# Gathering every second expert tile as quarter rows and turning it on VectorE in 32x32 blocks, in an attention and mixture-of-experts layer on one core

## Chip, core and metric

The kernel runs on one core of a Trainium2 chip. The metric is device time in microseconds (us) for one execution. The engines are TensorE (PE for its matmuls, PEld for its weight loads), VectorE (DVE), ScalarE (ACT), GpSimd (POOL) and the queue of SyncE (SP), which issues the plain DMAs. GpSimd issues the indirect DMAs, which gather rows by a list of row numbers.

## What is computed

One layer over 8 sequences of 512 tokens with 512 features: a layer norm, then the input plus causal attention with 16 heads plus a mixture of experts in which every token goes to 2 of 8 experts.

```python
x = L0_attn_x                                  # (8, 512, 512) float32
xn = _layernorm(x, axis=-1)
x = x + attn(xn, Wq, Wk, Wv, Wo) + ffn(xn, gate_w, expert_w, expert_b)

# ffn
xf = x.reshape(B * S, D)                       # 4096 tokens
gate_logits = xf @ gate_w.T                    # 8 experts
top_vals, top_idx = jax.lax.top_k(gate_logits, 2)
w = jax.nn.softmax(top_vals, axis=-1)
y_all = jnp.einsum('td,eod->teo', xf, expert_w) + expert_b[None, :, :]
y_sel = jnp.take_along_axis(y_all, top_idx[:, :, None], axis=1)
out = jnp.sum(y_sel * w[:, :, None], axis=1)
```

## The kernel before

The attention is done in 32 steps (a batch and four heads each). Between step 15 and step 16 stands the expert stage, which the change is about. By then VectorE has sorted the tokens: each of the 8192 choices of a token has a slot, the slots of an expert fill whole tiles of 128, and there are `NTILE` = 71 tiles. `tok_of` holds the token in every slot, `exp_of` the expert of every tile. The normalised input lies in memory as `xn_rows`, one row of 512 float32 (2 KB) for each token.

The loop over tiles `s` = 0 to 70 is a pipeline over five engines with four buffers of everything. Nothing in it is scheduled by a planner: each engine has its own program, written in a fixed order, and waits on semaphores.

- POOL, `gather_x(s)` (L603 to L611): one indirect DMA fetches the 128 rows of tile s into `x_g[s % 4]`. It waits until tile s-4 has been read from that buffer (`xg_turned`).
- PE, `turn_xg(s)` (L930 to L939, the transposes are at L926): four 128x128 float32 transposes of `x_g` into a PSUM bank.
- ACT, `high_xg(s)` (L786), reads that bank and writes the high float16 half of `x_gT`. DVE, `low_xg(s)` (L1439), subtracts and writes the low half.
- PE, `expert(s)` (L949): 12 matmuls of 128x512 float16 (four chunks of features, three products of halves) with the expert's weights `w_exp`, which lie on the chip for all 8 experts.
- DVE, `scale_y(s)` (L1453): scale and bias from the PSUM bank into `y_sb`. SP, `store_y(s)` (L526): the tile goes to `y_rows`.

TensorE's program in this stage is the transposes of tile s+1 and then the matmuls of tile s, and so on:

```python
for s in range(NTILE):
    if 0 < s < NTILE - 1:
        turn_xg(s + 1)
    expert(s)
```

VectorE's program is `low_xg(s + 3)` and then `scale_y(s)`, for each s. Because `low_xg(s + 3)` needs the transposes that TensorE makes just ahead of `expert(s + 2)`, VectorE runs about two tiles behind TensorE's matmuls with its `scale_y`. After the stage, POOL gathers the results of the experts back by token (`gather_y`, L620, two indirect DMAs of 128 rows of 2 KB for a tile of tokens), and steps 16 to 31 add them up.

Attention has a block transpose on VectorE already: `turn_blk` (L1429) turns 32x32 blocks of `x_blk` in place, and `normalise_o` has two more (L1499, L1501).

## Time and profile before

| | |
|---|---|
| time before, median of 3 runs | 984.97 us (984.73 to 988.17) |
| the profiled execution: its own time | 987.53 us |
| the profiled execution: its span, first to last instruction | 985.8 us |
| PE busy | 917.9 us, 93% |
| DVE busy | 744.3 us, 76% |
| POOL busy | 561.3 us, 57% |
| ACT busy | 436.6 us, 44% |
| granted clock of TensorE, mean | 0.987 |

The span is the time from the first to the last instruction of the profiled execution. Busy times are sums over the whole span, and they are averages over stages with different limits: the expert stage has to be read by itself, by the instructions of one tile in order of time.

### The profile page before, as it was taken

To read this page: it belongs to the slowest core of one execution; us is meant where nothing else is said; L and a number is where in the kernel's file an instruction comes from. 1 tells how busy PE (TensorE), PEld (TensorE's weight loads), DVE (VectorE), ACT (ScalarE), POOL (GpSimd) and SP (SyncE) were. 2 spreads that over 40 slices of the span, in tenths; PEclk is the share of its full clock that TensorE was granted. 3 is DMA by queue.
4 is the path that set the end of the run, shared out by engine and by line. 5 is a ranking of instruction groups with operands and counts; after the bars stand their busy time and mean duration, and the time that the engine had idled before them with its cause. 6 is when DMAs were issued, how large, how long until landed. Compare 5 with 4: busy or idle time off the path is not lost.

```text
span 985.8 us, 18723 instructions
## 1 busy us (share of the span) xinstructions
PE 917.9 (93%) x6557; PEld 452.1 (46%) x6589; DVE 744.3 (76%) x1327; ACT 436.6 (44%) x711; POOL 561.3 (57%) x553
## 2 busy tenths in 40 slices
PE   2898898999999989989999999989999999999887
PEld 1344344444444544545555555544444444444333
DVE  7988988898789899944444444487788888888865
ACT  5367867766765433431122111124334444344432
POOL 1545676674776446763333333157878888778731
PEclk9999999999999999999999999999999999999999
DMA  6365589688786353485655555464655554565531
GB/s 243 109 223 198 179 269 320 199 306 293 211 275 260 119 204 97 187 291 192 198 176 178 172 171 174 148 214 141 193 177 188 172 194 141 163 189 159 173 103 55
DMA packets 107963, 188.63 MB, mean 191 GB/s; under 512 B 11872, under 2 KB 65248, under 8 KB 102624
## 3 DMA queue, kind: packets, MB, share of 16 engines
q1 hardware_dynamic: 97072, 152.03, 44.4%
q0 software_dynamic: 10800, 35.40, 12.5%
q8 instruction: 56, 0.92, 0.4%
q14 instruction: 35, 0.29, 0.1%
HBM read 117.13 MB, written 70.25 MB: 190 GB/s over the span
## 4 chain that ended last, share of the span: by engine, by line
PE 66%; DVE 14%; DMA 6%; ACT 5%; POOL 4%; issue 3%; SPq 1%; another core or an unknown queue 0%; DVEq 0%; ACTq 0%; POOLq 0%
PE psum L949 19%; PE psum L1034 10%; PE psum L1058 7%; PE psum L997 5%; PE psum L984 5%; PE psum L966 5%; PE psum L1000 5%; PE psum L1043 4%; PE psum L926 4%; DVE top L1483 3%; ACT pT L762 2%; DMA sum_sb<-x 2%; POOL k_hl L590 1%; PE psum L968 1%; DMA w_rows<-w_hl 1%
## 5 line engine op out<-in xcount | busy, mean ns | idle before, releaser
L762 ACT ACTIVATE pT<-psum,factors 128x512 f32<-128x512 f32 (+1 forms) x352 | 218.2, 642 | 244.0 <-PE psum L984 226.8
L1483 DVE TENSOR_REDUCE top<-psum 128x1 f32<-128x384 f32 (+3 forms) x352 | 210.4, 634 | 22.0 <-PE psum L968 16.6
L1034 PE MATMUL psum<-xT,w_att 128*128 128x512 f16 x768 | 195.7, 380 | 6.7 <-DVE xT L1434 4.7
L949 PE MATMUL psum<-w_exp,x_gT 128*128 x852 | 195.3, 379 | 0.6 <-DVE x_gT L1439 0.6
L610 POOL DMA_INDIRECT x_g<-xn_rows,tok_of x71 | 67.5, 951 | 131.5 <-PE psum L926 129.6
L966 PE MATMUL psum<-k_stack,q_stack 96*128 96x384 f16 (+3 forms) x512 | 127.8, 303 | 15.6 <-DVE top L1483 13.0
L984 PE MATMUL psum<-q_stack,k_stack 98*128 98x256 f16 (+3 forms) x512 | 129.5, 306 | 11.0 <-ACT pT L762 8.9
L1439 DVE TENSOR_TENSOR x_gT<-psum,x_gT 128x512 f16<-128x512 f32 x71 | 49.0, 692 | 104.1 <-ACT x_gT L786 90.7
L949 PEld LDWEIGHTS psum<-w_exp,x_gT 128*128 128x128 f16 x852 | 83.4, 98 | 85.5 <-issue 0.9
L786 ACT ACTIVATE x_gT<-psum 128x512 f16<-128x512 f32 x71 | 42.3, 597 | 170.0 <-PE psum L926 170.0
L600 POOL TENSOR_TENSOR o_hl<-o_sb,o_hl 128x512 f16<-128x512 f32 x31 | 36.5, 1178 | 127.9 <-ACT o_hl L776 123.2
L1034 PEld LDWEIGHTS psum<-xT,w_att 128*128 128x128 f16 x768 | 70.0, 97 | 73.6 <-DVE xT L1434 5.1
L594 POOL TENSOR_SCALAR_AFFINE_SELECT pT<-pT 128x512 f32<-128x512 f32 x128 | 95.1, 753 | 11.7 <-ACT pT L762 11.6
L1058 PE MATMUL psum<-w_att,o_hl 128*128 128x512 f16 x384 | 100.2, 386 | 1.3 <-DVE o_hl L1520 1.3
L1043 PE MATMUL psum<-w_att,xT 128*128 128x512 f16 x384 | 98.1, 380 | 0.0
L997 PE MATMUL psum<-pT,v_sb 128*32 128x512 f32 (+1 forms) x992 | 92.7, 446 | 0.0
L1000 PE MATMUL psum<-pT,ones 128*32 128x512 f32 (+1 forms) x992 | 91.5, 441 | 0.0
L966 PEld LDWEIGHTS psum<-k_stack,q_stack 96*128 96x128 f16 x512 | 46.5, 98 | 69.1 <-DVE top L1483 32.0
L620 POOL DMA_INDIRECT y_in<-y_rows,idx_y x64 | 66.8, 1043 | 19.7 <-issue 11.6
L968 PE MATMUL psum<-causal,ident 128*128 128x128 bf16 (+1 forms) x320 | 74.2, 232 | 0.0
L984 PEld LDWEIGHTS psum<-q_stack,k_stack 98*128 98x128 f16 x512 | 44.3, 98 | 64.1 <-ACT pT L762 18.1
L585 POOL TENSOR_TENSOR turned_q<-turned_q,trig_sb 128x512 f32<-128x512 f32 x32 | 40.6, 1270 | 42.7 <-DVE plain_q L1468 42.7
(175 smaller groups left out, 1301.9 us busy)
## 6 DMA issues: line engine op xcount, KB each, us to landing
y_rows<-y_sb SPq DMA_DIRECT2D x71, 256.0 KB
w_in<-w_all SPq DMA_DIRECT2D x12, 1024.0 KB, 12.1
q_stack<-qk_rows SPq DMA_DIRECT2D x96, 128.0 KB
k_stack<-qk_rows SPq DMA_DIRECT2D x96, 128.0 KB
x_in<-x SPq DMA_DIRECT2D x8, 1024.0 KB, 10.2
qk_rows<-q_hl SPq DMA_DIRECT2D x32, 256.0 KB
qk_rows<-k_hl SPq DMA_DIRECT2D x32, 256.0 KB
xn_rows<-x_in SPq DMA_DIRECT2D x8, 1024.0 KB, 5.0
```

The source lines that it names most:

```text
L594: pool.affine_select(out=p_diagonal(j), in_=p_diagonal(j), compare_op=ALU.is_ge, fill=0.0, base=0, pattern=[[0, HG], [1, P]], channel_mult ...
L762: act.activation(p_of(j, h, heads), banks[BANK_T + (NT_ * n + k) % 2][:, 0:W], ACT.Exp, scale=factors[:, 0:1]).then_inc(exp_done, 1)
L949: now = pe.matmul(banks[s % 4], x_gT[s % 4][:, xp * C + c, :], w_exp[:, bass.ds(e, 1), wp, c, :].rearrange("p e d -> p (e d)"), start=n == ...
L966: pe.matmul(bank[:, h * W:(h + 1) * W], q_stack[u][0:ROW_C, h0 + h, i * P:(i + 1) * P], k_stack[u][0:ROW_C, h0 + h, 0:W], start=h == 0, st ...
L968: pe.matmul(bank[:, 0:heads * W].rearrange("p (h t) -> p h t", h=heads)[:, :, W - P:W], ident16[:], causal[:, 0:heads, :], start=False, st ...
L984: now = pe.matmul(bank[:, h * W:(h + 1) * W], k_stack[u][0:ROW_C + 2, h0 + h, j * P:(j + 1) * P], q_stack[u][0:ROW_C + 2, h0 + h, j * P:S] ...
L997: pe.matmul(banks[BANK_O][h * HD:(h + 1) * HD, j * P:S], v_sb[b % 2][:, j, g * P + h * HD:g * P + (h + 1) * HD], p_of(j, h, 1), start=j == ...
L1000: now = pe.matmul(banks[BANK_DEN][h * HD:(h + 1) * HD, j * P:S], ones32[:], p_of(j, h, 1), start=j == 0, stop=j == J - 1)
L1034: now = pe.matmul(bank, w_att[:, what, wp, c, g * P:(g + 1) * P], xT[b % 2][:, xp * C + c, :], start=at_pass == 0, stop=at_pass == 3 * C - 1)
L1043: now = pe.matmul(banks[bank], xT[b % 2][:, xp * C + c, j * P:(j + 1) * P], w_att[:, 2, wp, c, :], start=at_pass == 0, stop=at_pass == 3 * ...
L1058: now = pe.matmul(banks[bank], o_hl[b % 2][:, c, xp, j * P:(j + 1) * P], w_att[:, 3, wp, c, :], start=at_pass == 0, stop=at_pass == 3 * C - 1)
L1483: return dve.tensor_reduce(out=top[:, h:h + heads, i], in_=banks[BANK_S + k % 2][:, 0:heads * W].rearrange("p (h t) -> p h t", h=heads), a ...
```

## The change

Tiles 5, 7, 9, ... 69 (33 tiles, `BLK`) no longer go through TensorE's transposes. `xn_rows` is seen as quarter rows of 128 float32 (`xn_quarters`). For such a tile POOL issues four indirect DMAs instead of one. Each fetches 128 quarter rows of 512 bytes, so that partition q*32+r holds quarter q of 32 tokens. One `dve.transpose` in 32x32 blocks then turns the tile in place. ACT and DVE take the high and low halves from `x_g` itself, in SBUF, with a stride of four elements. The weights of the experts are laid out by the host so that the features match, and the transposes of the other tiles read with the same stride. The buffer `x_g` of such a tile comes free with `low_xg` and not with the transposes of TensorE.

The list of quarter rows (`tok_blk`) is made once: POOL builds a spreading matrix `four16` in step 13, TensorE spreads the tokens with four small matmuls ahead of tile 0 (`spread_tokens`), and VectorE writes the list (`block_tokens`).

```diff
+    FIRST_BLK = 5
+    BLK = list(range(FIRST_BLK, NTILE, 2))
...
+    xn_quarters = xn_rows.rearrange("t (a f) -> (t a) f", f=P)
...
             def gather_x(s):
                 u = s % 4
-                if s >= 4:
-                    pool.wait_ge(xg_turned, s - 3)
+                if s - 4 in BLK:
+                    pool.wait_ge(xg_lo, s - 3)
+                elif s >= 4:
+                    pool.wait_ge(xg_turned, rows_till(s - 4))
...
-                pool.indirect_dma_start(x_g[u][:], None, xn_rows, bass.IndirectOffsetOnAxis(ap=tok_of[:, s:s + 1], axis=0))\
-                    .then_inc(gathered[u], 16)
+                if s in BLK:
+                    if s == FIRST_BLK:
+                        pool.wait_ge(blk_done, 1)
+                    i = BLK.index(s)
+                    for t in range(P // HD):
+                        pool.indirect_dma_start(x_g[u][:, t * P:(t + 1) * P], None, xn_quarters,
+                                                bass.IndirectOffsetOnAxis(ap=tok_blk[:, t, i:i + 1], axis=0)).then_inc(gathered[u], 16)
+                else:
+                    pool.indirect_dma_start(x_g[u][:], None, xn_rows, bass.IndirectOffsetOnAxis(ap=tok_of[:, s:s + 1], axis=0))\
+                        .then_inc(gathered[u], 16)
...
+                if n == CHOOSE + 2:
+                    pool.wait_ge(chosen_done, 1)
+                    pool.tensor_copy(four16[:], ident16[:].rearrange("p (t r) -> p t r", r=HD).unsqueeze(2).broadcast_to([P, P // HD, C, HD]))\
+                        .then_inc(four_made, 1)
...
             def high_xg(s):
-                act.wait_ge(xg_turned, s + 1)
+                if s in BLK:
+                    act.wait_ge(xg_blocked, blks_till(s))
+                else:
+                    act.wait_ge(xg_turned, rows_till(s))
...
+                if s in BLK:
+                    act.activation(by_chunks(x_gT[s % 4][:, 0:C, :]), of_blocks(x_g[s % 4][:]), ACT.Copy).then_inc(xg_hi, 1)
...
+            def spread_tokens():
+                pe.wait_ge(four_made, 1)
+                pe.wait_ge(tok16_done, 1)
+                for t in range(P // HD):
+                    now = pe.matmul(banks[BANK_T + 1][:, t * len(BLK):(t + 1) * len(BLK)],
+                                    four16[:, t, :, :].rearrange("p a r -> p (a r)"),
+                                    tok16[:, FIRST_BLK:NTILE:2], start=True, stop=True)
+                now.then_inc(blk_spread, 1)
...
+            spread_tokens()
             for s in range(NTILE):
-                if 0 < s < NTILE - 1:
+                if 0 < s < NTILE - 1 and s + 1 not in BLK:
                     turn_xg(s + 1)
                 expert(s)
...
+                if s in BLK:
+                    hi, lo = (by_chunks(x_gT[s % 4][:, h * C:(h + 1) * C, :]) for h in range(2))
+                    dve.tensor_tensor(lo, of_blocks(x_g[s % 4][:]), hi, ALU.subtract).then_inc(xg_lo, 1)
...
+            def turn_xg_blocks(s):
+                dve.wait_ge(gathered[s % 4], got(s))
+                here = x_g[s % 4][:].rearrange("p (t r c) -> p t c r", c=C, r=HD)
+                dve.transpose(here, here).then_inc(xg_blocked, 1)
...
             def read_tokens():
                 dve.wait_ge(tok_summed, 1)
+                dve.tensor_copy(tok16[:], banks[BANK_QV][:, 0:NTILE]).then_inc(tok16_done, 1)
...
             for s in range(NTILE):
+                if s + 4 in BLK:
+                    turn_xg_blocks(s + 4)
                 if s + 3 < NTILE:
                     low_xg(s + 3)
```

On POOL, the place is the start of the expert stage. Before, the rows after `o_hl` are the gathers of tiles 4, 5, 6, 7 and 8, one DMA each:

```order
L600 TENSOR_TENSOR o_hl_105<-o_sb,o_hl_105 128x512 [waits o_hi]
L610 DMA x_g_120<-xn_rows,tok_of 128x512 [waits xg_turned]
L610 DMA x_g_121<-xn_rows,tok_of 128x512 [waits xg_turned]
L610 DMA x_g_122<-xn_rows,tok_of 128x512 [waits xg_turned]
L610 DMA x_g_123<-xn_rows,tok_of 128x512 [waits xg_turned]
L610 DMA x_g_120<-xn_rows,tok_of 128x512 [waits xg_turned]
```

With the change the same place reads as follows. The rows are those of tiles 4 to 7 (L649 is the line of a whole-row gather now, L646 that of the quarter rows, and `small_sb` holds the list `tok_blk`):

```order
L629 TENSOR_TENSOR o_hl_107<-o_sb,o_hl_107 128x512 [waits o_hi]
L649 DMA x_g_122<-xn_rows,tok_of 128x512 [waits xg_turned]
L646 DMA x_g_123<-xn_rows,small_sb 128x128 [waits blk_done,xg_turned]
L646 DMA x_g_123<-xn_rows,small_sb 128x128 x3
L649 DMA x_g_124<-xn_rows,tok_of 128x512 [waits xg_turned]
L646 DMA x_g_125<-xn_rows,small_sb 128x128 [waits xg_turned]
L646 DMA x_g_125<-xn_rows,small_sb 128x128 x3
```

Two tiles are five DMAs on POOL's queue where they were two. The gathers keep their order, and each whole-row gather stands behind the four of the tile ahead of it.

On DVE, the place is the first two turns of the loop. Before, after the last `normalise_o`, `low_xg(2)`, `low_xg(3)` and the scale of tile 0:

```order
L1504 TENSOR_TENSOR o_sb<-psum,rden 128x512 [waits o_lo,dve_own]
L1439 TENSOR_TENSOR x_gT_130<-psum,x_gT_130 128x512 [waits xg_hi]
L1439 TENSOR_TENSOR x_gT_131<-psum,x_gT_131 128x512 [waits xg_hi]
L1447 TENSOR_LOAD exp_of [waits bias_loaded]
L1447 ISA x2
L1453 ISA [waits q_stored,y_done]
L1453 SCALAR_TENSOR_TENSOR y_sb_124<-psum,down,bias_all 128x512
```

With the change there is the list of quarter rows (L1516) ahead of tile 2, and the block transpose of tile 5 (L1512) ahead of the low half of tile 4:

```order
L1583 TENSOR_TENSOR o_sb<-psum,rden 128x512 [waits o_lo,dve_own]
L1516 TENSOR_SCALAR small_sb<-psum,small_sb 128x132 [waits blk_spread]
L1507 TENSOR_TENSOR x_gT_132<-psum,x_gT_132 128x512 [waits xg_hi]
L1507 TENSOR_TENSOR x_gT_133<-psum,x_gT_133 128x512 [waits xg_hi]
L1526 TENSOR_LOAD exp_of [waits bias_loaded]
L1526 ISA x2
L1532 ISA [waits q_stored,y_done]
L1532 SCALAR_TENSOR_TENSOR y_sb_126<-psum,down,bias_all 128x512
L1512 STREAM_TRANSPOSE x_g_123<-x_g_123 128x4x4x32 [waits gathered1]
L1507 TENSOR_TENSOR x_gT_130<-psum,x_gT_130 128x512 [waits xg_hi]
```

So VectorE now waits for a gather itself, and while it waits for tile s+4, the low half of tile s+3 and the scale of tile s stand behind it.

## Rows read from the trace of the kernel before

**Rows 1.** The page, busy time of each engine over the span.

```profile
PE 917.9 (93%) x6557; PEld 452.1 (46%) x6589; DVE 744.3 (76%) x1327; ACT 436.6 (44%) x711; POOL 561.3 (57%) x553
```

**Rows 2.** Stretches of the expert stage: PE, PEld, DVE, ACT, POOL busy, PEclk, DMA, GB/s.

```profile
500.00:550.00 50.00, 50.00 (x266) 27.08 (x264) 24.18 (x34) 9.55 (x16) 15.35 (x17) 1.00 0.53 172
```

**Rows 3.** Timeline, about one tile in the steady state: start, us, instruction, idle before.

```profile
504.43 0.60 PE L926 MATMUL psum<-ident,x_g 128*128 128x128 f32 x4
...
504.87 2.75 PE L949 MATMUL psum<-w_exp,x_gT 128*128 x12
505.07 0.60 ACT L786 ACTIVATE x_gT<-psum 128x512 f16<-128x512 f32 x1 [2.43 <-PE psum L926]
505.30 0.95 POOL L610 DMA_INDIRECT x_g<-xn_rows,tok_of  x1 [2.08 <-PE psum L926]
505.70 0.69 DVE L1439 TENSOR_TENSOR x_gT<-psum,x_gT 128x512 f16<-128x512 f32 x1 [1.43 <-ACT x_gT L786]
506.54 0.75 DVE L1453 SCALAR_TENSOR_TENSOR y_sb<-psum,down,bias_all 128x512 f32<-128x512 f32 x1 [0.15 <-issue]
...
507.46 0.60 PE L926 MATMUL psum<-ident,x_g 128*128 128x128 f32 x4
...
507.89 2.75 PE L949 MATMUL psum<-w_exp,x_gT 128*128 x12
```

**Rows 4.** The chain that ended last, end of the stage: start, us, what.

```profile
641.23 5.19 PE psum L949 x24
```

**Rows 5.** Timeline of POOL at the start of the stage.

```profile
436.33 0.96 POOL L610 DMA_INDIRECT x_g<-xn_rows,tok_of  x1
437.60 0.95 POOL L610 DMA_INDIRECT x_g<-xn_rows,tok_of  x1 [0.30 <-issue]
438.85 0.95 POOL L610 DMA_INDIRECT x_g<-xn_rows,tok_of  x1 [0.30 <-issue]
```

**Rows 6.** Line L620, the gathers of y: duration in ns, then the time to landing.

```profile
L620 POOL DMA_INDIRECT y_in<-y_rows,idx_y x64: 945/978/1363, 650.3 to 953.8; - x64
...
DMA to landing us min/median/max: 3.3/3.6/4.2
```

**Rows 7.** The queues between 430 and 647 us: packets, MB, share of 16 engines.

```profile
q0 software_dynamic: 5446, 17.84, 28.4%
```

**Rows 8.** Tile x_blk: SP loads in 512-byte pieces, VectorE's block transpose, ScalarE's reading.

```profile
L1429 DVE STREAM_TRANSPOSE x_blk<-x_blk x24: 662/694/711, 115.7 to 282.0; 128x512 f32<-128x512 f32 x24
L718 ACT ACTIVATE gT<-x_blk x24: 612/612/631, 121.0 to 285.2; 128x512 f16<-128x512 f32 x24
...
DMA to landing us min/median/max: 3.7/4.7/6.9
```

**Rows 9.** Timeline of POOL: gathers beside VectorE's instructions of rows 10.

```profile
676.80 0.99 POOL L620 DMA_INDIRECT y_in<-y_rows,idx_y  x1 [0.27 <-POOL idx_y L618]
...
690.52 1.36 POOL L620 DMA_INDIRECT y_in<-y_rows,idx_y  x1 [0.27 <-POOL idx_y L618]
...
935.38 1.10 POOL L620 DMA_INDIRECT y_in<-y_rows,idx_y  x1 [0.31 <-issue]
```

**Rows 10.** Timeline of DVE at the same times.

```profile
677.35 0.71 DVE L1501 STREAM_TRANSPOSE rden<-rden_few 128x512 f32<-128x512 f32 x1
...
690.24 0.75 DVE L1528 SCALAR_TENSOR_TENSOR late_sb<-y_in,w,late_sb 128x512 f32<-128x512 f32 x1
...
934.92 0.75 DVE L1527 SCALAR_TENSOR_TENSOR late_sb<-y_in,w,late_sb 128x512 f32<-128x512 f32 x1
```

**Rows 11.** Timeline around the small additions: step 13, the token list, tile 0.

```profile
365.72 1.16 POOL L600 TENSOR_TENSOR o_hl<-o_sb,o_hl 128x512 f16<-128x512 f32 x1 [12.08 <-ACT o_hl L776]
...
406.55 0.23 DVE L1443 TENSOR_SCALAR tok_of<-psum 128x71 int32<-128x71 f32 x1 [0.77 <-PE psum L919]
...
432.22 2.76 PE L949 MATMUL psum<-w_exp,x_gT 128*128 x12 [0.61 <-DVE x_gT L1439]
...
444.33 2.75 PE L949 MATMUL psum<-w_exp,x_gT 128*128 x12
```

More of the change, by code:

```diff
@@ L89, in moe_attention_layer @@
     tile_no = small_sb[:, NT * E:NT * E + NTILE]
+    quarter = small_sb[:, NT * E + P:NT * E + P + 1]
     count16 = at("count16", [P, P], F16)
@@ L97, in moe_attention_layer @@
     tok_of = at("tok_of", [P, NTILE], I32)
+    tok16 = at("tok16", [P, NTILE], F16)
     exp_of = at("exp_of", [P, NTILE], I32)
@@ L114, in moe_attention_layer @@
     shift = at("shift", [P, 2, J], F32)
+    logit_at = place[0]
     logit = at("logit", [P, NT, E], F32)
+    four16 = at("four16", [P, P // HD, C, HD], F16, logit_at)
+    tok_blk = small_sb[:, 0:P // HD * len(BLK)].bitcast(I32).rearrange("p (t s) -> p t s", t=P // HD)
+    assert P // HD * len(BLK) <= NT * E and 2 * C * P <= 4 * NT * E
     best = at("best", [P, 2, NT], F32)
@@ L226, in moe_attention_layer @@
     tok_summed, tok_done, bias_loaded = sem("tok_summed"), sem("tok_done"), sem("bias_loaded")
+    four_made, tok16_done, blk_spread, blk_done, xg_blocked = (sem(n) for n in ("four_made", "tok16_done", "blk_spread", "blk_done", "xg_blocked"))
     gathered = [sem(f"gathered{u}") for u in range(4)]
@@ L288, in moe_attention_layer, with rows_till, blks_till, got @@
     HALF_LAST = [(BANK_O, BANK_DEN), (BANK_T, BANK_T + 1)]
+    def rows_till(s):
+        return s + 1 - blks_till(s)
+    def blks_till(s):
+        return len([i for i in BLK if i <= s])
+    def got(s):
+        return sum(64 if i in BLK else 16 for i in range(s % 4, s + 1, 4))
     def outs_till(n):
@@ L328, in by_blocks, with by_chunks, of_blocks @@
         return row.rearrange("p (t r) -> p t r", r=HD)
+    def by_chunks(part):
+        return part.rearrange("p c (t r) -> p c t r", r=HD)
+    def of_blocks(rows):
+        return rows.rearrange("p (t r c) -> p c t r", c=C, r=HD)
     def spread_at(i):
@@ L785, in high_xg @@
                     act.wait_ge(pv_done, J * N1)
-                act.activation(x_gT[s % 4][:, 0:C, :].rearrange("p c t -> p (c t)"), banks[BANK_QV + s % 4], ACT.Copy).then_inc(xg_hi, 1)
+                if s in BLK:
+                    act.activation(by_chunks(x_gT[s % 4][:, 0:C, :]), of_blocks(x_g[s % 4][:]), ACT.Copy).then_inc(xg_hi, 1)
+                else:
+                    act.activation(x_gT[s % 4][:, 0:C, :].rearrange("p c t -> p (c t)"), banks[BANK_QV + s % 4], ACT.Copy).then_inc(xg_hi, 1)
             def step(n):
@@ L938, in turn_xg @@
                     pe.wait_ge(o_read, N1)
-                turn_tile(x_g[s % 4][:], BANK_QV + s % 4).then_inc(xg_turned, 1)
+                rows = x_g[s % 4][:].rearrange("p (f c) -> p c f", c=C)
+                for k in range(C):
+                    now = pe.transpose(banks[BANK_QV + s % 4][:, k * P:(k + 1) * P], rows[:, k], ident32[:])
+                now.then_inc(xg_turned, 1)
             def expert(s):
@@ L945, in expert @@
                     pe.wait_ge(y_scaled, s - 3)
+                elif s == BANK_T + 1:
+                    pe.wait_ge(blk_done, 1)
                 n = 0
@@ L1714, in by_turned_features, with by_strided_features @@
         return w.T.reshape(C, C, P // C, w.shape[0]).transpose(0, 2, 1, 3).reshape(P, C, w.shape[0])
-    mats = [chunks(a["L0_ffn_expert_w"][e]) for e in range(E)]
+    def by_strided_features(w):
+        return w.T.reshape(P, C, w.shape[0])
+    mats = [by_strided_features(a["L0_ffn_expert_w"][e]) for e in range(E)]
     mats += [by_turned_features(a["L0_attn_" + n]) for n in ("Wq", "Wk", "Wv")] + [chunks(a["L0_attn_Wo"])]
@@ L1725 @@
     small = np.concatenate([np.tile(E - np.arange(E), T // P), np.arange(P)]).astype(np.float32)
+    small = np.tile(small, (P, 1))
+    quarter = (D // P * (T // 2) + np.arange(P)[:, None] // (P // C)).astype(np.float32)
     arrays = {
@@ L1731 @@
         "trig": trig,
-        "small": np.tile(small, (P, 1)),
+        "small": np.concatenate([small, quarter], axis=1),
     }
```

10 lines of the change are left out of this document (8 added, 2 removed).

## Prediction, made before the change was run

> **What bounds the kernel now.** I read the busy shares first, then the expert stage by itself. TensorE is busy for 93% of the span and VectorE for 76% [rows 1]. Those are averages over stages. In the middle of the expert stage PE is busy for 50.00 of 50 us at the full granted clock, VectorE for 24.18, ScalarE for 9.55 and POOL for 15.35, and the DMA engines for 0.53 [rows 2]. The timeline says what PE does. The matmuls of one tile begin at 504.87 and those of the next at 507.89, 3.02 us later. Four transposes begin at 504.43, 0.44 us before the matmuls, and at 507.46, 0.43 before [rows 3]. So a tile costs PE about 2.59 us of matmuls and 0.44 of transposes, and nobody keeps it waiting: POOL idles 2.08 us ahead of each gather, ScalarE 2.43. The stage runs from 432.22, where tile 0 begins [rows 11], to 641.23 + 5.19 = 646.42 [rows 4].
>
> **What goes from the path.** 33 tiles lose their transposes: 33 x 0.44 = 14.5 us. That is the ceiling of the gain. Two tiles would take 2 x 3.02 - 0.44 = 5.6 us of PE in place of 6.04. Everything else has to fit into 5.6 us for two tiles.
>
> **What is added on POOL.** Two tiles are five indirect DMAs where they were two. At the start of the stage three gathers go out with nothing to wait for. They begin at 436.33, 437.60 and 438.85, and each runs 0.95 us with 0.30 us of issue between them [rows 5]. A gather thus takes POOL 1.25 us. The gathers of y are of the same kind, 128 rows of 2 KB, with a median of 0.978 us [rows 6]. Five of them are 6.25 us for two tiles. This is more than the 5.6 of PE with the change, and more than the 6.04 of today. POOL's average of 57% hides it, since it waits for most of each tile now.
>
> The open price is that of a quarter-row gather. No row shows one of 512-byte rows. From above I take 1.25 us, because the number of rows (128) and of indices is the same and the work of making the descriptors goes by these. Of a lower price I can only say that 0.30 us of issue stays. If the busy part went by bytes it would be 0.95 / 4 = 0.24, so that the lower end is 0.54 us. I take 1.25. The Trainium skill (DMA: Bandwidth & Descriptors, "Anatomy of one DMA — SWDGE (gpsimd) path") calls descriptor generation "small, variable" and says that many descriptors can be emitted before it shows, with some 2.0 us fixed for a DMA. By the page alone POOL would not be the limit and the sum would be the gain of the second case below; the 0.95 us of the row is what this kernel pays, so I go by the row.
>
> **The sum.** POOL begins tile 4 at 436.33 as before. Until the last quarter of tile 69 it starts 1 gather for tile 4, 33 x 4 = 132 quarters and 32 whole ones for tiles 6 to 68. The last of these 165 starts 164 x 1.25 = 205.0 us later, at 641.33. It lands 3.6 us after its issue [rows 6], at 644.9. VectorE then turns the tile in 0.69 [rows 8] and makes the low half of tile 68, which stands behind that transpose on its queue, in 0.69 [rows 3]. With about 0.06 for each semaphore tile 68 can begin at 646.5. Three tiles of matmuls and one set of transposes follow, 3 x 2.59 + 0.44 = 8.2, so the stage ends at 654.7, against 646.42: **+8.3 us**. It begins at once: the last quarter of tile 5 starts at 441.3 and lands at 444.9, and the low half of tile 4 follows at 446.4, where PE wanted it at 444.33 [rows 11].
>
> **VectorE beside POOL.** Half of the low-half subtractions now read two tensors in SBUF (x_g and the high half). A gather beside such an instruction is longer. One took 1.36 us (0.95 otherwise) where L1528 had begun 0.28 us before it and ran 0.47 us into it; one took 1.10 where L1527 ran 0.29 us into it [rows 9, 10]. The block transpose from SBUF to SBUF (L1501) does not do this: the gather at 676.80 took 0.99 [rows 9, 10]. There is one such subtraction for two tiles. When it falls between the starts of two gathers it costs nothing, and when it lies over one as in the worst row it costs 0.41. I take 0.15, near the row in which a third of a microsecond overlaps: 33 x 0.15 = **+5.0 us**, between 0 and 13.5. The Trainium skill (SBUF — State Buffer, "SBUF: two separate sides") gives a rule for it: the one of VectorE and GpSimd that comes second is blocked until the other's instruction ends. The trace agrees roughly. By the rule at its worst it would be the whole 0.69 us each time, 22.8 us in all, which no row here shows.
>
> **What is hidden.** The block transpose (0.69) makes VectorE's work for two tiles 24.18 / 50 x 6.04 + 0.69 = 3.6 us [rows 2], well under 6.25, and ScalarE's reading from SBUF takes 0.61 [rows 8], as from PSUM. If either were twice as long it would still fit. The spreading matrix on POOL in step 13 lies in the 12.08 us that POOL waits there [rows 11]. The four small matmuls ahead of tile 0 fall into the 0.61 us that PE waits for x_gT [rows 11]. The one small copy ahead of `tok_of` is on PE's path: 0.15 to 0.23 us [rows 11], say **+0.15**. The DMA engines: a gather of 256 KB now takes 0.284 x 16 x 217 / 67 = 14.7 engine-us, 0.92 us of all sixteen [rows 7]. In small pieces it may be twice that, 1 us more in 6.25, on a share of 0.53: no bound.
>
> In all 8.3 + 5.0 + 0.15 = +13.4 us. On the profiled execution that is a span of 985.8 + 13.4 = 999.2, with 1.7 us around it. The median lies 2.6 us below that execution's time, so the forecast is 984.97 + 13.4 = **998.4 us**.
>
> **The cases.**
> - *POOL is the bound* (0.67). 993.4 with no collision between VectorE and POOL, 1006.9 with the worst row at each pair. For it speaks the pitch of 1.25 us; against it only that quarter rows were not seen.
> - *Cheap quarter gathers* (0.15), the other sign: POOL keeps up and PE stays the bound. This decides at the price of one gather. The stage is even with today's at 1.25 - 8.3 / 164 = 1.20 us a gather without a collision, and PE is the bound from about 5.6 / 5 = 1.12 us down. At 1.0 us or less the gain is 14.5 less about 2 for the wait for tile 5's quarters at the start: 972.5 us. For it speaks that only a quarter of the bytes is described.
> - *In between* (0.06): a pitch of 1.16 to 1.21 us, 980 to 990.
> - *The ring is too short* (0.12). A quarter tile holds its buffer for three pitches (3.75), the landing, the transpose, the low half of the tile ahead, the scale and its own low half, about 7 us besides the landing. Four buffers give it two pairs, 12.5 us, so up to a landing of 5.5 us it costs nothing. Loads in 512-byte pieces landed in 3.7, 4.7 and 6.9 us at the least, the median and the most [rows 8]. At the median nothing changes but 1 us at the end; at 6.9 a pair would take (7 + 6.9) / 2 = 6.95 us, 0.7 more, and the time would be 1016 to 1022. A sign of this would be gaps on POOL.
>
> **How the numbers follow.** A measurement of this kernel tells about 0.5%, 4.9 us, from no change. Faster than 980 us: the second case and a little of the third, 0.16. Between 980 and 990: the rest of the third and a sliver of the first, 0.06. Slower: the first and the fourth, 0.78. The range goes from 986 to 1015 us: it holds the first case with its bounds of 0 and 13.5 us, half of the third, and the milder half of the fourth, about 0.8 in all, and leaves the second out.
>
> **What would show it.** In the stage, gathers of quarter rows on POOL at a pitch of 1.25 us with "issue" in front of each and no wait for PE or DVE; POOL near 76% busy there; PE with a wait of about half a microsecond or more ahead of every second tile, released by DVE's low half; two tiles in 6.3 to 6.6 us where it was 6.04; a wait of VectorE for the gathers' landing; PE and the clock elsewhere as before. A wrong first step would be a quarter gather clearly under 0.95 us busy. A wrong second step would be POOL waiting for `xg_lo` or for PE in the middle of the stage. A granted clock of 1.2 GHz in the stage, where it is 2.4 now, would make it worse than all of these.

## The result and the profile after

The change made the kernel slower: 1011.95 us (median of 4 runs, 1007.78 to 1015.55) against 986.57 us (median of 4 runs, 984.73 to 990.37). The ratio is 1.0242, 95% interval 1.0201 to 1.0284, which is about +23.9 us (the two medians lie 25.4 us apart). The forecast was 998.4 us, +13.4. The direction and the range (986 to 1015) held, the size of the change did not. The profiled execution took 1015.55 us, the most of the four, so what is read from its trace below is the costly end of what this kernel does.

The page of the changed kernel, span and busy times:

```profile
span 1013.8 us, 18572 instructions
## 1 busy us (share of the span) xinstructions
PE 915.7 (90%) x6429; PEld 441.1 (44%) x6461; DVE 783.9 (77%) x1362; ACT 454.2 (45%) x711; POOL 671.0 (66%) x653
```

TensorE is busy for 2.2 us less and the span is 28 us longer. POOL went from 57% to 66% [rows 1]. Part 4 of the same page, the chain that ended last by line:

```profile
POOL x_g L646 11%; PE psum L1097 10%; PE psum L1121 6%; PE psum L1060 5%; PE psum L1047 5%; PE psum L1029 5%; PE psum L1063 4%; PE psum L1012 4%; PE psum L1106 4%; DVE top L1562 3%; POOL x_g L649 3%; DMA c_rows<-c_turn 2%; DMA x_blk<-xn_rows 1%; POOL gT L610 1%; PE psum L1031 1%
```

The gathers of quarter rows (L646) head the chain now. In the kernel before, the expert matmuls (L949) stood there with 19%, and no gather of x_g was among the first lines. The matmuls (L1012) have shrunk to 4%.

```profile
PE psum L949 19%; PE psum L1034 10%; PE psum L1058 7%; PE psum L997 5%; PE psum L984 5%; PE psum L966 5%; PE psum L1000 5%; PE psum L1043 4%; PE psum L926 4%; DVE top L1483 3%; ACT pT L762 2%; DMA sum_sb<-x 2%; POOL k_hl L590 1%; PE psum L9
```

The timeline of POOL at the start of the stage, in the changed kernel, answers to [rows 5]:

```profile
444.19 0.97 POOL L649 DMA_INDIRECT x_g<-xn_rows,tok_of  x1
445.46 0.94 POOL L646 DMA_INDIRECT x_g<-xn_rows,small_sb  x1 [0.30 <-issue]
446.71 0.94 POOL L646 DMA_INDIRECT x_g<-xn_rows,small_sb  x1 [0.30 <-issue]
447.96 0.94 POOL L646 DMA_INDIRECT x_g<-xn_rows,small_sb  x1 [0.30 <-issue]
449.20 0.94 POOL L646 DMA_INDIRECT x_g<-xn_rows,small_sb  x1 [0.30 <-issue]
450.45 0.95 POOL L649 DMA_INDIRECT x_g<-xn_rows,tok_of  x1 [0.30 <-issue]
...
460.53 1.75 POOL L646 DMA_INDIRECT x_g<-xn_rows,small_sb  x1 [0.30 <-issue]
```

A gather of 512-byte rows takes 0.94 us, one of 2 KB rows 0.95, and both have 0.30 us of issue in front. POOL's pitch is 1.25 us and it waits for nobody. The last row is one of the gathers that took longer, 1.75 us. In the timeline of VectorE of the changed kernel at that time stands what ran beside it:

```profile
458.10 1.14 DVE L1512 STREAM_TRANSPOSE x_g<-x_g 128x512 f32<-128x512 f32 x1 [1.73 <-DMA x_g<-xn_rows,small_sb]
459.12 0.66 DVE L1507 TENSOR_TENSOR x_gT<-psum,x_gT 128x512 f16<-128x512 f32 x1
459.69 0.75 DVE L1532 SCALAR_TENSOR_TENSOR y_sb<-psum,down,bias_all 128x512 f32<-128x512 f32 x1
460.44 1.08 DVE L1505 TENSOR_TENSOR x_gT<-x_g,x_gT 128x512 f16<-128x512 f32 x1
461.43 0.74 DVE L1532 SCALAR_TENSOR_TENSOR y_sb<-psum,down,bias_all 128x512 f32<-128x512 f32 x1
```

The subtraction with two inputs in SBUF (L1505) began at 460.44, 0.09 us before the gather, and ended at 461.52. The gather ended at 462.28, 0.76 us after it. So the gather had done about 0.2 us of its work beside or before the wait and the rest afterwards: it lost 0.8 us. Where L1505 begins after the start of a gather, the gather takes 0.94. Here is such a pair, POOL and VectorE:

```profile
467.57 0.94 POOL L646 DMA_INDIRECT x_g<-xn_rows,small_sb  x1 [0.30 <-issue]
467.63 1.07 DVE L1505 TENSOR_TENSOR x_gT<-x_g,x_gT 128x512 f16<-128x512 f32 x1
```

This holds through the whole stage. From 450 us on, 25 gathers took longer than 0.98 us. Each had begun inside a subtraction L1505, and each ended 0.76 to 0.78 us after it. Two more began inside one and were not longer, one 0.03 us after the subtraction's start and one near its end. The 13 gathers in which a subtraction began took 0.94 to 0.95. Those subtractions took 1.06 to 1.08 us like all others, with no idle time in front: VectorE was never held up.

These are the groups of the stage, by line and form (engine, operation, count, busy, mean ns, idle before):

```profile
L646 POOL DMA_INDIRECT x_g<-xn_rows,small_sb x132 | 139.4, 1056 | 40.2 <-issue 40.2
L649 POOL DMA_INDIRECT x_g<-xn_rows,tok_of x36 | 34.9, 970 | 10.7 <-issue 9.9 <-PE psum L999 0.6
...
L1512 DVE STREAM_TRANSPOSE x_g<-x_g 128x512 f32<-128x512 f32 x33 | 37.3, 1130 | 83.9 <-DMA x_g<-xn_rows,small_sb 83.9
L1505 DVE TENSOR_TENSOR x_gT<-x_g,x_gT 128x512 f16<-128x512 f32 x33 | 35.4, 1073 | 0.1
```

The quarter gathers have a mean of 1056 ns and a median of 944 (below, with the third experiment). 132 x 0.112 = 14.8 us went into the gathers that were held up, and 36 x 0.024 = 0.9 more into those of whole rows. POOL's idle time here is its own issue, all but 0.6 us behind PE. VectorE's transpose and subtraction take 1.13 and 1.07 us where the forecast had 0.69 for each: both read x_g with a stride of four elements. The granted clock of TensorE was 0.99 in the mean from 440 to 678 us, the level of 2.4 GHz for nearly all of the stage, so a lower clock is not what made it long.

TensorE in the changed kernel, the line of the expert matmuls (first and last start, then what it waited for):

```profile
L1012 PE MATMUL psum<-w_exp,x_gT x852: 378/379/635, 440.4 to 677.6; 128*128 x171
...
  issue: 46.5, 42
  DVE x_gT L1507: 28.3, 20
```

From the first to the last of these matmuls it is 237.2 us. In the kernel before it was 646.0 - 432.2 = 213.8 us (432.22 in [rows 11], and the last matmul starts 0.4 before the end, 646.42, of [rows 4]). That is +23.4 us in the stage. The rest of this text calls this distance "the stage". The stage also begins 8.2 us later than before. From the start of the last matmul to the end of the span it is 3.6 us less than before (336.2 and 339.8). The experiments ask which part of this is the change.

### The profile page after: what moved, and what is told of

The parts are those of the page before. It is cut to its first block, busy times and chain, and to the rows that moved or that the text cites. A ratio compares the mean times of both kernels' runs of the same rounds, so it can differ in the third digit from the quotient of the medians.

```text
span 1013.8 us, 18572 instructions
## 1 busy us (share of the span) xinstructions
PE 915.7 (90%) x6429; PEld 441.1 (44%) x6461; DVE 783.9 (77%) x1362; ACT 454.2 (45%) x711; POOL 671.0 (66%) x653
## 4 chain that ended last, share of the span: by engine, by line
PE 48%; POOL 18%; DVE 15%; issue 7%; DMA 5%; ACT 4%; SPq 1%; another core or an unknown queue 0%; DVEq 0%; ACTq 0%; POOLq 0%
POOL x_g L646 11%; PE psum L1097 10%; PE psum L1121 6%; PE psum L1060 5%; PE psum L1047 5%; PE psum L1029 5%; PE psum L1063 4%; PE psum L1012 4%; PE psum L1106 4%; DVE top L1562 3%; POOL x_g L649 3%; DMA c_rows<-c_turn 2%; DMA x_blk<-xn_rows 1%; POOL gT L610 1%; PE psum L1031 1%
## 5 line engine op out<-in xcount | busy, mean ns | idle before, releaser
L1012 PE MATMUL psum<-w_exp,x_gT 128*128 x852 | 197.7, 384 | 29.1 <-DVE x_gT L1507 28.3
L646 POOL DMA_INDIRECT x_g<-xn_rows,small_sb x132 | 139.4, 1056 | 40.2 <-issue 40.2
L1012 PEld LDWEIGHTS psum<-w_exp,x_gT 128*128 128x128 f16 x852 | 84.2, 99 | 128.1 <-issue 45.9
L1047 PE MATMUL psum<-q_stack,k_stack 98*128 98x256 f16 (+3 forms) x512 | 129.2, 304 | 10.5 <-ACT pT L805 8.1
L1512 DVE STREAM_TRANSPOSE x_g<-x_g 128x512 f32<-128x512 f32 x33 | 37.3, 1130 | 83.9 <-DMA x_g<-xn_rows,small_sb 83.9
L835 ACT ACTIVATE x_gT<-psum 128x512 f16<-128x512 f32 x38 | 22.6, 597 | 110.2 <-PE psum L999 110.2
## 6 DMA issues: line engine op xcount, KB each, us to landing
x_in<-x SPq DMA_DIRECT2D x8, 1024.0 KB, 10.5
```

The costliest lines, as they stand in the source:

```text
L646: pool.indirect_dma_start(x_g[u][:, t * P:(t + 1) * P], None, xn_quarters, bass.IndirectOffsetOnAxis(ap=tok_blk[:, t, i:i + 1], axis=0)).t ...
L1012: now = pe.matmul(banks[s % 4], x_gT[s % 4][:, xp * C + c, :], w_exp[:, bass.ds(e, 1), wp, c, :].rearrange("p e d -> p (e d)"), start=n == ...
L1047: now = pe.matmul(bank[:, h * W:(h + 1) * W], k_stack[u][0:ROW_C + 2, h0 + h, j * P:(j + 1) * P], q_stack[u][0:ROW_C + 2, h0 + h, j * P:S] ...
```

## Experiments

Each kernel below was compared with the kernel before on the same chip. That kernel's median was 987.6 to 988.9 us in these comparisons, so the ratios, not the times, compare one experiment with another.

**e1: the kernel before, again.** No edit.

> The kernel before, run again with a profile of its own. In the two profiles so far tile 0 of the expert stage begins at 432.22 us before and at 440.39 us with the change, 8.2 us of the lost time ahead of the stage. If that is chance of an execution (landing times of DMAs in steps 3 to 10), this profile may show tile 0 anywhere from 432 to 440 us; if the change causes it, tile 0 is within 1 us of 432.2 here and near 440 in every kernel with the changed memory layout. The ratio is 1.000 within 0.4%.

Ratio 1.0029 (1.0003 to 1.0056), tile 0 at 435.26 us. Two things follow. The start of the stage moves by 3 us (432.2 and 435.3) between executions of one and the same kernel. And an identical kernel can come out 0.3% off, so a single difference of 0.3% shows nothing here.

**e2: quarter gathers replaced by whole ones.** It leaves out the right place of the rows, so the values of the 33 tiles are other than the reference's.

```diff
-                    i = BLK.index(s)
-                    for t in range(P // HD):
-                        pool.indirect_dma_start(x_g[u][:, t * P:(t + 1) * P], None, xn_quarters,
-                                                bass.IndirectOffsetOnAxis(ap=tok_blk[:, t, i:i + 1], axis=0)).then_inc(gathered[u], 16)
+                    pool.indirect_dma_start(x_g[u][:], None, xn_rows, bass.IndirectOffsetOnAxis(ap=tok_of[:, s:s + 1], axis=0))\
+                        .then_inc(gathered[u], 16)
```

> The changed kernel, but each tile of BLK is fetched by one indirect DMA of whole rows and not by four of quarter rows; the VectorE transpose, the list of quarter rows and everything else stay. The rows then stand in the wrong partitions for the transpose, so the values of these tiles are not the reference's. Theory POOL (the gathers' pitch of 1.25 us, with the stretched ones, is what ends last): POOL needs 2.5 us for two tiles, PE is the bound again with 5.65 us for two tiles, the stage takes 200 to 203 us where it takes 237.6, and the time is 970 to 976 us. Rival VectorE (its transposes of 1.13 us, the strided subtraction of 1.08 us and ScalarE's strided 1.13 us make the lateness): these stay, PE still waits ahead of every second tile, and the time stays above 995 us.

980.57 us, ratio 0.9932 (0.9902 to 0.9962). The line of the matmuls in this kernel, and that of the gathers of the 33 tiles:

```profile
L1010 PE MATMUL psum<-w_exp,x_gT x852: 379/379/387, 440.0 to 640.6; 128*128 x171
...
  issue: 1.2, 2
```

```profile
L644 POOL DMA_INDIRECT x_g<-xn_rows,tok_of x33 | 31.1, 941 | 72.6 <-DVE x_gT L1503 72.0 <-issue 0.6
```

The stage is 200.6 us, 13.2 less than before, and PE waits 1.2 us in all of it. VectorE's long transposes (median 1135 ns) and subtractions (1067 ns) are all still there, and POOL is the one that waits now, for VectorE. So the five gathers for two tiles make the loss in the stage, and the transposes on VectorE are covered. How much of it is their number and how much the held-up ones, e2 does not say, since both went. The theory of VectorE falls. The time of 980.6 was above the 970 to 976 expected, though, and the excess lies ahead of the stage, which begins at 440.0.

**e3: the block transpose writes to PSUM.** Every second tile as in the change, with four gathers.

```diff
             def turn_xg_blocks(s):
...
-                dve.transpose(here, here).then_inc(xg_blocked, 1)
+                there = banks[BANK_QV + s % 4].rearrange("p (c t r) -> p t c r", c=C, r=HD)
+                dve.transpose(there, here).then_inc(xg_blocked, 1)
```

`high_xg` and `low_xg` read the bank for these tiles too, and `gather_x` waits for `xg_blocked` where it waited for `xg_lo`.

> The changed kernel, but VectorE's block transpose writes into the PSUM bank that TensorE's transposes would have written. ScalarE and VectorE then read contiguous PSUM as for the other tiles, and VectorE has no instruction with two inputs in SBUF in this stage. The gathers stay as they are. Theory collision: the gathers of 1.5 to 1.8 us go, all of them take 0.94 to 0.95, two tiles take 6.25 us, the stage 222 to 224 us (14 to 16 less than with the change), and the time is 993 to 999 us. Rival ring (the landing and the waits on VectorE set the pace, the long gathers only fill a wait): the long gathers go, POOL shows waits in their place, and the time falls by less than 5 us.

998.01 us, ratio 1.0117 (1.0075 to 1.0159). The line of the gathers, in the changed kernel and in this one (duration min/median/max):

```profile
L646 POOL DMA_INDIRECT x_g<-xn_rows,small_sb x132: 940/944/1798, 445.5 to 664.7; - x132
```

```profile
L646 POOL DMA_INDIRECT x_g<-xn_rows,small_sb x132: 940/944/954, 439.5 to 643.1; - x132
...
L1009 PE MATMUL psum<-w_exp,x_gT x852: 379/379/388, 434.3 to 656.6; 128*128 x171
```

The longest gather fell from 1798 to 954 ns, and the stage from 237.2 to 222.3 us. That is 14.9 us, nearly the 15.7 us of surplus in the gathers. What is left, 222.3 - 213.8 = 8.5 us, is the forecast's first term (8.3). The theory of the ring falls: POOL kept its pace, and the waits for landing did not take the place of the long gathers. This version also gives the buffer back sooner. That is not the gain, since POOL hardly waited for a buffer in the changed kernel either (0.6 us).

**e4: only every third tile, transposed to PSUM.**

```diff
-    BLK = list(range(FIRST_BLK, NTILE, 2))
+    BLK = list(range(FIRST_BLK, NTILE, 3))
```

> As the transpose into PSUM, but only every third tile (5, 8, ... 68, 22 tiles) is gathered as quarter rows. Three tiles cost POOL 6 x 1.25 = 7.5 us and PE 3 x 3.03 - 0.44 = 8.65 us. Theory POOL: PE is the bound, the stage takes 214 - 22 x 0.44 = 204.5 us and up to 2 more at its start, and the time is 975 to 979 us, faster than before. Rival: the gathers' landing or VectorE keeps PE waiting ahead of every third tile all the same, and the time is 984 us or more.

987.19 us, ratio 0.9986 (0.9965 to 1.0007), where 975 to 979 us was expected. The stage is 643.8 - 435.9 = 207.9 us where 204.5 to 206.5 was expected. POOL waits for PE here, and PE hardly waits. The timeline of PE at the start of this kernel's stage shows where the rest went:

```profile
442.00 2.75 PE L1009 MATMUL psum<-w_exp,x_gT 128*128 x12
444.59 0.63 PE L996 MATMUL psum<-ident,x_g 128*128 128x128 f32 x4
445.06 2.75 PE L1009 MATMUL psum<-w_exp,x_gT 128*128 x12
449.79 2.76 PE L1009 MATMUL psum<-w_exp,x_gT 128*128 x12 [1.98 <-DVE x_gT L1500]
```

A tile with transposes takes 445.06 - 442.00 = 3.06 us and not 3.02: the transposes read x_g with the stride and take 0.63 - 0.60 = 0.03 us more, on every tile that keeps them. The wait of 1.98 us is that of tile 4, behind the quarters of tile 5, as forecast. The gain in the stage, 5.9 us, is in the trace, but the time was not below that of before. The profiled execution (983.06 us, the fastest of ten) had tile 0 at 435.9. That the others lost the gain ahead of the stage was a guess at this point, and the next experiments test it.

**e5: the additions alone.**

```diff
-    BLK = list(range(FIRST_BLK, NTILE, 2))
+    COLS = list(range(FIRST_BLK, NTILE, 2))
+    BLK = []
```

with `len(COLS)` in the making of the list.

> All that the change adds around the tiles, but no tile goes the new way: the spreading matrix in step 13, the float16 copy of the tokens, the four small matmuls, the list of quarter rows, the expert weights in their new order and TensorE's transposes with the stride of four elements; every tile is gathered whole and transposed by TensorE. The strided transposes cost 3.06 us a tile in place of 3.03 (read from the starts of the tiles with the change), 71 x 0.03 = 2.2 us. Theory chance: the later start of the expert stage (440.4 and 440.0 us in two of four changed kernels, 432.2 and 435.3 in the two profiles of before) is chance of an execution, and the time is 2 to 3 us above before. Rival systematic: something in these additions makes steps 3 to 10 slower, the stage begins at 436 to 440 us, and the time is 5 to 9 us above before.

996.92 us, ratio 1.0081 (1.0062 to 1.0101), +8.0 us, with tile 0 at 438.2 us and a stage of 654.3 - 438.2 = 216.1 us. The stage holds 2.3 us of it, the stride in TensorE's transposes. This is the rival's number. The rest, over 5 us, is not chance.

**e6: the memory layout alone.** No instruction is added.

```diff
+    tok16 = at("tok16", [P, NTILE], F16)
...
-        "small": np.tile(small, (P, 1)),
+        "small": np.concatenate([np.tile(small, (P, 1)), np.zeros((P, 1), np.float32)], axis=1),
```

> The kernel before, with only the memory layout of the change: the unused 160 bytes for the float16 tokens in each partition, which move every later tile in SBUF, and one more column in the array of small constants, which moves what lies behind it in memory. No instruction is added. Theory chance: no difference, 0.997 to 1.003. Rival systematic by layout: the stage begins near 438 us and the time is 3 us or more above before.

993.29 us, ratio 1.0051 (1.0033 to 1.0069), tile 0 at 437.98. The rival held. The two lines move every later tile of SBUF by 192 bytes in each partition, 160 for `tok16` and 32 for the longer `small_sb`.

**e7: two tiles of five, to PSUM, from tile 8 on.** With the list of tiles made of two lists with a step of 5.

```diff
-    FIRST_BLK = 5
-    BLK = list(range(FIRST_BLK, NTILE, 2))
+    FIRST_BLK = 8
+    PARTS = [list(range(FIRST_BLK + k, NTILE, 5)) for k in (0, 2)]
+    BLK = PARTS[0] + PARTS[1]
```

> Two tiles of five (8, 10, 13, 15, ... 70, 26 tiles) as quarter rows, turned into PSUM, from tile 8 on in place of tile 5. Five tiles cost POOL 11 x 1.25 = 13.75 us and PE 5 x 3.06 - 2 x 0.47 = 14.36 us. Theory POOL: PE is the bound, the stage has no stall near tile 4, and takes 71 x 3.06 - 26 x 0.47 = 205 us, 9 less than before; the time is 976 to 984 us by what the steps ahead of the stage do. Rival ring: the share of POOL (96%) leaves no room for landing and queue, PE waits ahead of many tiles, and the stage takes 212 us or more.

983.48 us, ratio 0.9945 (0.9924 to 0.9966). The stage is 646.3 - 441.6 = 204.7 us, as expected, 9.1 less than before, with the shifted layout still in it.

**e8: no stride.** The three instructions read x_g in order, so the features of these tiles are in the wrong order and the values are other than the reference's.

```diff
-        return rows.rearrange("p (t r c) -> p c t r", c=C, r=HD)
+        return rows.rearrange("p (c t r) -> p c t r", c=C, r=HD)
...
-                here = x_g[s % 4][:].rearrange("p (t r c) -> p t c r", c=C, r=HD)
+                here = x_g[s % 4][:]
```

> The changed kernel with every second tile, turned in place in SBUF, but VectorE's transpose, ScalarE's copy and VectorE's subtraction read x_g without the stride of four elements, so the features of these tiles are in another order than the weights want and the values are not the reference's. Theory collision by length: the three instructions fall from 1.13, 1.13 and 1.08 us to about 0.69, 0.61 and 0.69; the subtraction with two inputs in SBUF still holds up a gather, but by at most 0.45 us instead of 0.85, and the stage is 229 to 233 us where it was 237.6 (and 222 with the transpose into PSUM). Rival: the stride costs in itself, as lateness on VectorE, and not by the gathers; then the stage falls to 224 us or less.

1005.81 us, ratio 1.0165 (1.0137 to 1.0192). Groups of this kernel in the stage:

```profile
L646 POOL DMA_INDIRECT x_g<-xn_rows,small_sb x132 | 129.7, 983 | 40.2 <-issue 40.2
...
L1512 DVE STREAM_TRANSPOSE x_g<-x_g 128x512 f32<-128x512 f32 x33 | 23.5, 711 | 104.7 <-DMA x_g<-xn_rows,small_sb 104.7
L1505 DVE TENSOR_TENSOR x_gT<-x_g,x_gT 128x512 f16<-128x512 f32 x33 | 22.3, 677 | 0.0
```

Without the stride the subtraction takes 0.68 us, and the surplus in the quarter gathers is 132 x 0.039 = 5.1 us in place of 14.8. This is near the forecast's 5.0 us. The stage is 668.9 - 442.9 = 226.0 us, less than the 229 to 233 expected and more than the rival's 224. Against the change the stage lost 11.2 us and the gathers' surplus 10.5, so the held-up gathers explain nearly all of it, and I had set them too high here.

**e9 and e10: the two halves of the layout.** The pad of 160 bytes alone, and the column in memory alone (not loaded).

```diff
+    tok16 = at("tok16", [P, NTILE], F16)
```

```diff
-            sp.dma_start(small_sb[:], small).then_inc(const_in, 16)
+            sp.dma_start(small_sb[:], small[:, 0:small.shape[1] - 1]).then_inc(const_in, 16)
```

> The kernel before with only the unused 160 bytes in each partition of SBUF, half of the layout shift that cost 0.51%. If the place of the tiles in SBUF is the cause: 1.003 to 1.007 and the stage begins near 438 us. If the array of constants is: 0.998 to 1.002.

> The kernel before with only the one more column in the array of small constants in memory, which is not loaded; SBUF is as before. If the place of the arrays in memory is the cause of the 0.51%: 1.003 to 1.007. If it is the place of the tiles in SBUF: 0.998 to 1.002.

The pad: 1.0037 (1.0015 to 1.0058), tile 0 at 438.90. The column: 1.0006 (0.9988 to 1.0023), tile 0 at 432.90. This speaks for the place in SBUF, but by the ratio alone the pad is hardly more than what e1 gave for no edit, and the start of tile 0 is a weak witness. Over all profiles it lies between 434.3 (e3) and 442.9 (e8) with the shifted tiles, and between 432.0 (e14) and 436.0 (e11) with the tiles in place or shifted by 256 bytes. The landings are a better one. Tile x_blk (512-byte pieces loaded by SP), time to landing in the kernel with the pad and in the one with the column:

```profile
DMA to landing us min/median/max: 3.7/5.5/7.7
```

```profile
DMA to landing us min/median/max: 3.4/4.9/7.7
```

**e11: the change with the layout of before.** `tok16` takes the place of `best`, and the number of the quarter is computed on the chip.

```diff
-    tok16 = at("tok16", [P, NTILE], F16)
...
+    tok16 = at("tok16", [P, NTILE], F16, best_at)
...
+            own.link(pool.iota(quarter_i, [[0, 1]], base=D // P * (T // 2) * (P // C), channel_multiplier=1))
...
+            own.link(dve.tensor_scalar(quarter_i, quarter_i, 5, None, ALU.logical_shift_right))
+            own.link(dve.tensor_copy(quarter, quarter_i))
```

> The changed kernel with the memory layout of before: the float16 tokens lie in a tile that is free by then, and the number of the quarter is made on the chip (one iota on POOL, two small VectorE instructions at the start) and not loaded. Theory two causes: the change without the shift of layout loses 4 to 6 us less, 1.017 to 1.021, and the expert stage itself is as long as with the change, 236 to 239 us. Rival: the layout matters only for the kernel before, and the ratio stays at 1.023 or more.

1008.95 us, ratio 1.0192 (1.0157 to 1.0227), within the expectation. The stage was 668.8 - 436.0 = 232.8 us, 4.4 less than with the change, which I had not expected. Its gathers say why:

```profile
L648 POOL DMA_INDIRECT x_g<-xn_rows,small_sb x132 | 134.7, 1021 | 40.2 <-issue 40.2
L651 POOL DMA_INDIRECT x_g<-xn_rows,tok_of x36 | 35.2, 979 | 10.7 <-issue 9.9 <-PE psum L1001 0.6
```

The surplus is 132 x 0.077 + 36 x 0.033 = 11.4 us and not 15.7. In this trace 18 gathers took longer than 0.98 us, in that of the change 25. How many are caught depends on how the two programs meet. With one trace of each kernel it stays open whether that goes with the kernel or with the execution.

**e12: two tiles of five, to PSUM, with the layout of before.** The edits of e7 and e11 together.

> Two tiles of five as quarter rows, turned into PSUM, from tile 8, with the memory layout of before. Theory two causes: the 4 to 6 us of the layout come on top of the gain of 0.55% measured with it, 0.987 to 0.991, 976 to 979 us. Rival: no more gain than with the shifted layout, 0.993 to 0.996.

979.09 us (977.44 to 981.82), ratio 0.9905 (0.9879 to 0.9931), at the upper end of what was expected. This version is faster than both kernels, about 9 us under the one before. Its matmuls and its gathers:

```profile
L1014 PE MATMUL psum<-w_exp,x_gT x852: 378/379/387, 435.0 to 638.8; 128*128 x171
...
  issue: 1.8, 3
```

```profile
L649 POOL DMA_INDIRECT x_g<-xn_rows,small_sb x104 | 98.1, 944 | 40.7 <-issue 27.7 <-PE psum L1001 12.9
```

PE waits 1.8 us in a stage of 203.8 us, and POOL waits for PE now.

**e13 and e14: pads of 128 and 256 bytes.** The kernel before with `place[0] += 128` (256) ahead of `exp_of`.

> The kernel before with 128 unused bytes in each partition. The pads so far were 160 bytes (ratio 1.0037) and, in the full layout shift, 160 + 32 = 192 bytes (1.0051); neither is a multiple of 128, and in both the loads of x_blk landed in 5.5 us where they land in 4.7 to 4.9 with the layout of before. Theory alignment to 128 bytes: 0.998 to 1.002, x_blk in 4.7 to 4.9 us. Rival any shift: 1.003 or more.

> The same with 256 bytes. Theory alignment to 128 bytes: 0.998 to 1.002. If 256 is the step that matters and not 128, this one is at 1.000 and the pad of 128 bytes is not. Rival any shift: both at 1.003 or more.

128 bytes: 1.0029 (1.0008 to 1.0050), x_blk landing in a median of 5.0 us. 256 bytes: 1.0009 (0.9992 to 1.0026), x_blk in 4.8. The pad of 256 bytes shows no loss, so it is not any shift that costs. For 128 bytes the ratio is no larger than that of e1 and tells nothing, but the traces do. These are the plain DMAs' packets, MB and share of the 16 DMA engines between 100 and 300 us: before, with the pads of 128 and 256 bytes, and with that of 160 (e9):

```profile
q1 hardware_dynamic: 34928, 51.51, 77.2%
```

```profile
q1 hardware_dynamic: 35085, 50.63, 79.0%
```

```profile
q1 hardware_dynamic: 35037, 51.78, 77.6%
```

```profile
q1 hardware_dynamic: 34791, 49.30, 79.8%
```

A share of 77.2% of 16 engines for 200 us, divided by 51.51 MB, is 48.0 us of one engine for a MB. It is 49.9 with 128 bytes, 48.0 with 256 and 51.8 with 160. The same rows of all seventeen traces fall into groups that do not touch: 48.0 to 48.4 in the seven kernels with the tiles in place or shifted by 256 bytes, 51.2 to 51.8 in the nine with 160 or 192 bytes, and 128 bytes between them. So with 160 or 192 bytes the DMA engines work about 7% longer for the same bytes, and in this measure 128 bytes costs half as much (one trace). What 128 bytes cost in time stays open.

**e15: every second tile, to PSUM, with the layout of before.** The edits of e3 and e11.

> The change with the transpose into PSUM (no held-up gathers) and with the memory layout of before: what is left is the pitch of the gathers alone. By the forecast's own term for the pitch, +8.3 us, with 0.03 us for each of 38 strided TensorE transposes hidden under POOL: 1.007 to 1.010. If POOL's pitch were not the bound then: 1.003 or less.

995.17 us, ratio 1.0070 (1.0046 to 1.0094). The stage is 654.4 - 432.5 = 221.9 us, +8.1.

## Why the prediction was wrong, step by step

- **The bound and its term: right.** "A gather thus takes POOL 1.25 us" held to the hundredth for quarter rows (0.94 + 0.30). The term was +8.3 us; the two kernels without held-up gathers gave +8.5 (e3) and +8.1 us (e15) in the stage, and e15's time is +0.70% (0.46 to 0.94), 6.9 us. POOL was busy for 38.7 of the 50 us from 480 us, 77% where 76% was named as the sign. PE's waits were fewer and longer than named, 28.3 us at 20 starts and not half a microsecond at every second tile. The wait of tile 4 came as described, and e2 shows that two gathers in place of five turn the loss into a gain. The sentence of the Trainium skill that descriptor generation is small and shows only late (DMA: Bandwidth & Descriptors, "Anatomy of one DMA — SWDGE (gpsimd) path") did not carry here: 0.94 us of POOL for each DMA, with rows of 512 bytes or of 2 KB, is what set the pace.
- **"33 x 0.15 = +5.0 us, between 0 and 13.5": this is the step that failed.** The surplus was 15.7 us in the profiled execution and 11.4 in that of e11. As time it is 1.0192 - 1.0070, 1.2% or 12 us (e11 against e15; with their intervals 8 to 16 us). The mechanism was right and its size was off by more than two times. The bound for one pair, 0.41 us, was too low as well. It came from a gather beside an instruction of 0.75 us that had begun 0.28 us earlier, and here a gather lost up to 0.85 us. The new subtraction takes 1.07 us, since it reads x_g with a stride of four elements, and it often begins just ahead of a gather. So the row of 0.69 us for `low_xg` was the wrong one: it was taken from a contiguous PSUM operand for a strided SBUF operand.
- **How the size could have been worked out.** The forecast took its 0.15 by eye from the overlap. What the traces show is when a held-up gather ends: 0.76 to 0.78 us after the subtraction. The rows of before had this already, with 0.81 and 0.89 us [rows 9, 10]. A gather that begins d us after the subtraction's start then loses 1.07 - d + 0.77 - 0.94 = 0.90 - d. If the subtractions fell anywhere in the pitch of 1.25 us alike, that would be 0.32 us each, 33 x 0.32 = 10.7 us. With 0.68 us and the 0.81 of e8's trace it would be 0.12 each, 4.0 us. These are estimates from the rows named, near the 11.4 of e11 and the 5.1 of e8. So the length of the subtraction explains most of the miss. The 15.7 of the change has bad luck in it: 13 of its 25 long gathers began within 0.1 us of a subtraction's start. That e8 met the forecast's 5.0 is luck in part too, since 0.15 was not worked out from a length.
- **"The block transpose from SBUF to SBUF does not do this": right, but its row did not show it.** The transpose of [rows 10] began 0.55 us after the gather, and a gather that begins first loses nothing in any case. The changed kernel does show it: 17 gathers began inside a transpose L1512 and took 0.94 to 0.95 us.
- **The Trainium skill's rule on the shared ports** (SBUF — State Buffer, "SBUF: two separate sides") gave 22.8 us at its worst with 0.69 us. For a gather that comes second the trace agrees with it more closely than I had allowed: the gather ends 0.76 us after the subtraction, nearly its whole duration. The other half of the rule, as the prediction put it, did not show: a subtraction that began inside a gather took 1.06 to 1.08 us, with no idle time in front.
- **"What is hidden": half right.** The longer transposes and ScalarE's copy (1.13 us each and not 0.69 and 0.61) were covered, as e2 and the sums of e8 show. The stride in TensorE's own transposes, 0.03 us a tile, was not in the sum. It is hidden behind POOL in the change and costs where PE is the bound.
- **Not in the prediction at all: the layout.** I looked for instructions and missed what an added tile does to the others. This term stood at nothing. Four pairs of kernels that differ only in it, or almost only, give +0.50% (change and e11), +0.47% (e3 and e15), +0.40% (e7 and e12) and +0.51% (e6 and before), +4 to 5 us. Each of the first two differences alone is no clearer than about 0.5 points either way. The last two are clear of noise, and the four agree.
- **The rivals.** Cheap quarter gathers: excluded by 0.94 us. The ring: excluded by POOL's idle time, all issue but for 0.6 us.

In per cent of the time the loss is 0.70 for the pitch (e15), 1.22 for the held-up gathers (e11 less e15) and 0.50 for the layout (change less e11). These are differences along one row of kernels and give the 2.42 by the way they are made, so their sum proves nothing. What supports them is what each was measured by besides: the stage of e3 and e15, the surplus in the gathers, and e6. Against the forecast's terms the pitch came out 1.4 us lower, the held-up gathers some 7 us higher, and the layout 5 us where there was no term.

Why the place of the tiles in SBUF matters is open in part. Between 100 and 300 us the DMA engines work 51.2 to 51.8 us for a MB where it costs, and 48.0 to 48.4 where it does not. The landings of x_blk are longer too (medians of 5.2 to 5.8 us, against 4.7 to 5.0). No run shows which tiles matter, or why the engines take longer.

## What to carry to other kernels

Count gathers by the number of DMAs on GpSimd's queue and not by bytes: here each costs 1.25 us back to back, and the share of tiles that can be split follows from that (two of five fit, every second does not). When GpSimd is the bound, keep long VectorE instructions with two SBUF inputs from beginning ahead of its gathers. Here the transpose written to PSUM, so that the subtraction had only one input in SBUF, was worth about 12 us. And add small tiles where they don't move the large ones, and run a kernel with the new layout alone before a loss of half a per cent is put down to the new instructions.

## What the runs showed of the hardware

- An indirect DMA of 128 rows costs GpSimd the same for rows of 512 bytes and of 2 KB: median 944 and 946 ns, and 0.30 us of issue.
- A stride of four float32 in SBUF makes VectorE's 128x512 block transpose 1.13 us (0.71 without, e8), the subtraction 1.07 us (0.68), and ScalarE's copy 1.13 us (0.63 without, e8). TensorE's four transposes take 0.03 us more.
- A gather that begins inside a VectorE subtraction with two SBUF inputs ends 0.76 to 0.78 us after it (0.81 to 0.83 in e8) and takes up to 1.80 us, where it takes 0.94 alone (25 gathers of the changed kernel; one that began 0.03 us after the subtraction was not held up). A gather that begins ahead of the subtraction takes 0.94 to 0.95, and the subtraction keeps its 1.06 to 1.08 us.
- A VectorE block transpose that reads a strided SBUF tile and writes PSUM takes 1.11 us, one that writes SBUF 1.13, and a gather beside either stays at 0.94 to 0.95 us.
- With the later SBUF tiles shifted by 160 or 192 bytes in each partition the plain DMAs take 51.2 to 51.8 us of one DMA engine for a MB between 100 and 300 us, with 128 bytes 49.9, in place or with 256 bytes 48.0 to 48.4. The time is 0.37% (160 bytes, e9) and 0.51% longer (192, e6), and 0.09% within noise with 256 (e14).
